# Second edge pass of a two-layer graph network: four gathers to a group behind three landings, no gate between pairs

## The reference

```python
q = (X @ Wq)[src]                       # [E, 64]
k = (X @ Wk)[dst]
e = jnp.tanh(q + k)
scores = e @ Wphi
exp_scores = jnp.exp(scores - jnp.max(scores))
denom = jax.ops.segment_sum(exp_scores, src, num_segments=N)
alpha = exp_scores / (denom[src] + 1e-09)
vy = (X @ Wy_w + Wy_b)[dst]
msg = alpha[:, None] * (vy + e @ We)
out = jax.ops.segment_sum(msg, src, num_segments=N)
# called with edge_index = stack([src, dst]); before it: x = layernorm(x + L0(x, ...))
x = layernorm(x + out)
```

## Time and profile before

| | us |
|---|---|
| median of 3 runs (lowest, highest) | 3570.61 (3570.06, 3587.74) |
| the profiled execution | 3560.17 |
| its span | 3558.5 |
| PE busy (matmul) | 2677.2 (75%) |
| DVE busy | 1794.6 (50%) |
| ACT busy | 1547.0 (43%) |
| POOL busy | 1665.1 (47%) |

### The profile page before, as it was taken

How to read it: one execution, slowest core, us unless ns; L and a number is a source line. 1 busy time by engine, 2 the same in 40 slices (tenths; PEclk the granted TensorE clock), 3 DMA queues, 4 the chain that set the end, 5 groups by cost and what they waited for, 6 DMA issues and landing times. The chain is left out here.

```text
span 3558.5 us, 71246 instructions
## 1 busy us (share of the span) xinstructions
PE 2677.2 (75%) x17372; PEld 1866.4 (52%) x17372; DVE 1794.6 (50%) x5675; ACT 1547.0 (43%) x4560; POOL 1665.1 (47%) x1723
## 2 busy tenths in 40 slices
PE   5899999599877888787889536666666666666764
PEld 4344443376655665565667325555555555555552
DVE  8934521255434343433345625555555565565564
ACT  2677777355333333333345113444444444344342
POOL 0355554211565566655630045555555555555540
PEclk9999999799877777778779556666677676676666
DMA  8333333355433333333321122222222222222220
GB/s 96 90 104 105 107 117 108 105 158 150 125 99 100 98 101 98 99 97 101 102 91 35 30 62 67 62 64 64 63 64 64 67 63 64 64 64 65 63 55 18
DMA packets 321792, 297.80 MB, mean 84 GB/s; under 512 B 196992, under 2 KB 249237, under 8 KB 321680
## 3 DMA queue, kind: packets, MB, share of 16 engines
q0 software_dynamic: 72320, 160.26, 16.8%
q1 hardware_dynamic: 249360, 136.30, 13.9%
HBM read 191.89 MB, written 25.22 MB: 61 GB/s over the span
## 5 line engine op out<-in xcount | busy, mean ns | idle before, releaser
L1566 POOL DMA_INDIRECT sum_acc<-kv_table,rec_all x784 | 783.3, 999 | 605.6 <-issue 217.1
L1056 POOL DMA_INDIRECT area_b<-h_table,src_g x544 | 564.3, 1037 | 373.7 <-remote 143.9
L1629 PE MATMUL bank<-sum_acc,probT 128*128 128x193 f32 x1760 | 554.3, 484 | 153.9 <-DVE probT L1757 112.4
L1629 PEld LDWEIGHTS bank<-sum_acc,probT 128*128 128x128 f32 x1760 | 455.2, 285 | 218.1 <-DVE probT L1757 138.1
L1126 PE MATMUL bank<-hs,y_sb 128*128 128x129 f32 x2400 | 410.6, 326 | 45.5 <-ACT y_sb L1149 41.1
L715 ACT ACTIVATE sum_acc<-bank,bias 128x512 f32<-128x512 f32 x588 | 360.2, 709 | 133.5 <-PE bank L586 125.4
L1153 ACT COPY y_sb<-bank 128x512 f32<-128x512 f32 x300 | 175.5, 585 | 555.1 <-remote 271.6
L1126 PEld LDWEIGHTS bank<-hs,y_sb 128*128 128x128 f32 x2400 | 376.6, 238 | 56.6 <-ACT y_sb L1149 51.0
L501 POOL DMA_INDIRECT early<-h_table,src_g x240 | 237.6, 990 | 344.9 <-ACT sum_acc L715 267.0
L1240 DVE SCALAR_TENSOR_TENSOR sum_acc<-sum_acc,shrink,bank 128x129 f32 x300 | 104.8, 349 | 567.6 <-remote 275.7
L586 PE MATMUL bank<-area_b,wc 64*128 64x512 f32 x1176 | 342.1, 632 | 3.7 <-ACT sum_acc L715 3.7
(11 more groups left out here) (287 smaller groups left out, 4638.8 us busy)
## 6 DMA issues: line engine op xcount, KB each, us to landing
hs<-area_b SPq DMA_DIRECT2D x300, 258.0 KB
area_b<-in_edge_attr SPq DMA_DIRECT2D x97, 256.0 KB
rows_table<-early POOLq DMA_DIRECT2D x60, 258.0 KB
area_b<-rows_table POOLq DMA_DIRECT2D x60, 258.0 KB
sum_acc<-kv_table,rec_all POOLq DMA_INDIRECT x784
qb<-q_table SPq DMA_DIRECT2D x220, 48.0 KB
area_b<-h_table,src_g POOLq DMA_INDIRECT x544
hbT<-hT_table SPq DMA_DIRECT2D x300, 16.0 KB
```

What stands on the lines that cost most here:

```text
L1056: pool.indirect_dma_start(out=landed_rows[:, k * GT + j, 0:D], out_offset=None, in_=h_table, in_offset=bass.IndirectOffsetOnAxis(ap=src_g[ ...
L1566: pool.indirect_dma_start(out=landed_rows[:, g % RING1 * GT + j, :], out_offset=None, in_=kv_table, in_offset=bass.IndirectOffsetOnAxis(ap ...
L1629: last = pe.matmul(bank[4 + k % 2][0:BN, 0:KV + 1], probT_v[:, k % 2, j, :], row_v[:, k % RING, j, AD:RK], start=(j == 0), stop=(j == GT - 1))
```

## The change

The two pairs become one loop of four gathers behind the wait for `stepped`; the wait for `hotT_done` is gone. The first three gathers of a group increment a new semaphore (`most_in`, one for even groups and one for odd), the fourth alone increments `landed`. Behind its four gathers POOL reports the group in front (`arrived(g - 1)`), and then waits until three gathers of the group just issued have landed (`three_in(g)`) before it goes on to the next group. This holds for the first 8 groups as well.

```diff
-                    def gather(g, pair):
+                    def gather(g):
                         pool.sem_inc(ticks, 1)
-                        for j in (2 * pair, 2 * pair + 1):
+                        for j in range(GT):
                             pool.indirect_dma_start(
                                 out=landed_rows[:, g % RING1 * GT + j, :], out_offset=None, in_=kv_table,
-                                in_offset=bass.IndirectOffsetOnAxis(ap=rec_all[:, g, 2 * j + 1:2 * j + 2], axis=0)).then_inc(landed[g % 4], 16)
+                                in_offset=bass.IndirectOffsetOnAxis(ap=rec_all[:, g, 2 * j + 1:2 * j + 2], axis=0)).then_inc(landed[g % 4] if j == GT - 1 else most_in[g % 2], 16)
 
                     def arrived(g):
-                        pool.wait_ge(landed[g % 4], 64 * (g // 4 + 1))
+                        pool.wait_ge(landed[g % 4], 16 * (g // 4 + 1))
                         pool.sem_inc(ready, 1)
+
+                    def three_in(g):
+                        pool.wait_ge(most_in[g % 2], 48 * (g // 2 + 1))
 
                     for g in range(GROUPS):
                         if g >= RING1:
                             at = GROUPS + (g - RING1) % 2 * GH + (g - RING1) // 2
                             last_step = pool.value_load(reach_row[0:1, at:at + 1], min_val=0, max_val=STEPS - 1)
                             pool.wait_ge(stepped, last_step + SU + 1)
-                        gather(g, 0)
-                        if g >= RING1:
-                            pool.wait_ge(hotT_done, last_step + 5)
-                        gather(g, 1)
+                        gather(g)
                         if g:
                             arrived(g - 1)
+                        three_in(g)
                     arrived(GROUPS - 1)
```

More of the change, by code:

```diff
@@ L1485, in build @@
             landed = [sem4(f"landed1_{k}") for k in range(4)]
+            most_in = [sem4(f"most_in1_{k}") for k in range(2)]
             ready = sem4("ready1")
```

## The result

The changed kernel has a median of 3483.55 us (3474.27 to 3491.16, 4 runs) against 3576.01 (3570.06 to 3587.74, 4 runs): a ratio of 0.9743, with an interval of 0.9716 to 0.9769, or 92 us faster. The forecast was 3540, 30 us less than the 3570.61 it started from. The sign was right; the size was too small by a factor of three.

The account below looks back on a forecast made before the run. It took the second edge pass to be paced by gather chains that hold PE's semaphores until their release. −60 + 43 − 12 = −29 took 3560.17 to 3531; plus 10.4 for the median, 3542, rounded to 3540; range 3460 to 3640.

Parts of the forecast that it names:

- What bounds the kernel before: Second edge pass: a loop of chain, release, consumers, next chain, with PE's semaphores held during gathers; 7.10 us per group.
- The wait for three landings: POOL's new wait after each group's gathers: hidden behind the wait for the finished step, so it costs nothing.
- a floor of 6.57: Shortest cycle by the semaphores' release: 0.80 + 4.71 + 1.06 us; the messages' floor of 6.78 was larger and held.
- Four gathers and always a pause, +43: Second pass: chains of six vanish, so 24 steps without a group cost 1.8 us each; 43 us slower, bounds 0 to 87.
- The dropped gate, −60: Gate on L1681 gone: chains start 0.80 instead of 1.37 after T, the waiting copy's start; 7.10 to 6.78, 60 us saved.
- The start, −12: First eight groups: pauses among 32 gathers let SP and PE through, so first messages end sooner; −12 us, between −18 and +4.
- The clock: Rival: a shorter cycle keeps PE near 2.4 GHz and messages take 1.57 us; 69 us faster, 3502; chance 0.13.
- The held top: Rival: L1623's handshake falls into the chain and is held, 3.6 us more per hit; 20 more hits give 3613; chance 0.28.
- The landings alone as the pace: Rival: consumers keep up and the landings set a cycle of 5.9 us; 226 us less, 3345; chance 0.05.

Follow-up runs that it names:

- two sets: Changed kernel with the second pass's message matmuls issued twice: 3503.33 us, ratio 0.9809 to the kernel before, which took 3575.64 on that chip.
- the kernel with the early load: Changed kernel with the next group's load of last_step moved in front of the wait for landings: 3123.06 us, ratio 1.0672 to the kernel before.

## Why the prediction was wrong in size

**What bounds the kernel before: right, for its chip, but for the odd steps.** The cycle of chain, release, consumers and next chain paces it; 7.10 per group where semaphores are held, 5.30 where they aren't, with the gate in the code both times. But the mean of 7.10 was read as 7.14 with the steps without a group absorbed. The cycles are 6.70 in the mean of 166, and 9.07 to 11.36 in the 21 others: these steps were paid for there.

**The wait for three landings, "behind the wait for the step it costs nothing": this step of the mechanism failed.** The wait is the pace of the changed kernel. Its terms were nearly right: a chain start 5.4 to 5.9 behind the last one was forecast and 5.96 measured, and 0.4 allowed for the load where 0.43 to 0.60 was measured. Their sum is the 6.54 of the cycle shown, with a mean of 6.71; the forecast had at most 5.9 + 0.4 = 6.3 for it, held it against a floor of 6.57 that came from the release, and let the maximum of the two decide. The few tenths that were missing turned the order round. The floors of 6.57 and 6.78 stand on a chain that waits for the messages' semaphore, and in the changed kernel that had come at least 9.5 us before every chain. The third gather's 0.95 us in the trace is not its data: it began at 2074.53 and POOL went on at 2077.97. The Trainium skill (Perfetto Trace Analysis, "DMA Instruction — SWDGE (GPSIMD)") says that the profiler's end of such an instruction is when the descriptors have been generated, not when the data have moved; the trace agrees, with 2.49 us between the two.

**Four gathers and always a pause, +43: this is the term of the sum that failed, by its sign.** I took the 24 steps without a group as absorbed before and let each pay 1.8 us after, as if the consumers did one step per cycle. It is the other way round: before, their long cycles cost 77 us; after, they cost nothing, because POOL no longer waits for the consumers and these have slack (220 steps in 196 cycles, and still 176.0 us of waiting for rows). The steady part as a whole was forecast at −60 + 43 = −17 and came out at −71.7, which is −77 for these steps and +5 for all other cycles.

**The dropped gate, −60: not seen.** The ordinary cycle took 6.70 before and 6.72 after. That −60 taken alone is near −71.7, and 6.78 near 6.71, is luck: neither comes from the reason given for it (the messages end, then 0.80). That 6.70, set by the chain and its release, and 6.72, set by POOL's loop with the landings, are so close is chance too.

**The start, −12: −6.0 at POOL, and −11.8 at the tail, which had no term.** The first messages ended 28 us sooner, as forecast (before 2115; it was 2097.73), but the consumers' lead isn't worth its size: POOL sets the end. It shows behind the last gather, where fewer steps are left over.

**The rivals.** The clock rose only from 0.68 to 0.72, and with it at 0.91 (two sets) the changed kernel was not quicker: not the cause. The held top did not come: its waits fell from 45 to 5, and no cycle of 11 us came, while the kernel before had such cycles already. The landings alone as the pace was the right mechanism, at chance 0.05, because I priced its cycle at 5.9 without the load. At 6.5 it gives 0.6 x 188 = 113 us less, nearer the truth than the forecast.

**What stays open.** Which part gives the gain on a holding chip, the dropped gate or the forced pause, was tried only on free chips. The trace favours the pause (six-gather chains and POOL's waits of up to 14.7 us gone, the top in time, the consumers ahead of the step that POOL asks for), but that is argued and not shown. Nor was the kernel with the early load run on a holding chip, where it could be the fastest of all; on free chips no kernel tried beats the one before. Why a step without a group costs 2.4 to 4.7 us when handshakes are held was not taken apart. And why chips differ isn't known, nor whether one chip always behaves the same.

## What to carry to other kernels

Price a new wait as a whole loop of the engine that carries it (its own work, the landing, the register work behind it), and compare that loop with the present cycle at its upper end; within a few per cent, treat the new wait as the pace. Steps that don't need the paced resource are then free. Before taking a mean as the cycle, list the cycles: here a mean close to the plain cycle hid 21 long ones, and they were the whole gain of the steady part. Measure a change that paces one engine on more than one chip: this one gains 2.6% where handshakes are held and lost 9.5% on the chip where they weren't.

## What the runs showed of the hardware

- The same program takes 2924 us on four chips and 3576 on another (and in the recorded pair). In the second edge pass it is 5.30 against 7.10 us per group. In the trace of the slow kind a handshake from PE to ACT that falls well into a chain of indirect gathers on POOL waits it out. The copy L1681 had 86 waits for "remote" of over 2 us in this pass there, and 65 of them ended 1.0 to 1.2 us behind a gather's end, in a pause. Early in a chain it passes at once (0.03 us in the cycle of the earlier trace rows). On a free chip it takes 0.04 us in mid-chain.
- SP shows it too. In the steady part of the changed kernel 71 of its 412 rows of a DMA's issue are about 0.7 us long in the recorded pair, and none of 414 is on the free chip. One of the kernel before on a free chip, and two in chains of the changed kernel in the recorded pair:

```profile
2201.26 0.33 SPq L1537 DMA_DIRECT2D qb<-q_table  x1
```

```profile
2704.70 0.72 SPq L1538 DMA_DIRECT2D qb<-q_table  x1
...
2710.56 0.72 SPq L1537 DMA_DIRECT2D rec_sb<-rec  x1
```

- On the holding chip, a second set of message matmuls raised the granted clock of the steady part from 0.68 to 0.87 in the kernel before, and 220 further sets cost 51 us in all, where they are at least 345 us of matmuls (1.57 us each).
